# One-core cross-attention block: the small passes of four engines moved between the steps of the attention loop

## What is computed

```python
def layer_norm(x, w, b):
    mu = jnp.mean(x, axis=-1, keepdims=True)
    var = jnp.mean(jnp.square(x - mu), axis=-1, keepdims=True)
    return (x - mu) * jax.lax.rsqrt(var + EPS) * w + b
residual = hidden_states
x = layer_norm(hidden_states, ln1_w, ln1_b)
q = (x @ q_w + q_b)                       # (B, H, LQ, HD) after the turn; k, v from the context
scores = jnp.einsum('bhqd,bhkd->bhqk', q, k) * scale
scores = jnp.where(mask, scores, mask_value)
attn = jax.nn.softmax(scores, axis=-1)
out = jnp.einsum('bhqk,bhkd->bhqd', attn, v)
out = out @ cproj_w + cproj_b             # heads side by side again
hidden = out + residual
residual = hidden
y = layer_norm(hidden, ln2_w, ln2_b)
y = jax.nn.gelu(y @ fc_w + fc_b, approximate=True)
return residual + (y @ proj_w + proj_b)
```

## Time and profile before

| | us |
|---|---|
| median of 3 runs | 833.96 (829.85, 833.96, 834.24) |
| the profiled execution, whole | 829.58 |
| its span, first to last instruction | 827.8 |
| projections, until the first s2 of the loop | 154.3 |
| attention loop | 298.7 |
| MLP | 375 |

### The profile page before, as it was taken

The page is one execution under the profiler, slowest core; times in us unless marked ns, Lnnn a source line. Parts: engine busy times, 40 slices in busy tenths (PEclk is TensorE's granted clock), DMA queues, the critical chain, the costliest instruction groups (busy, mean ns, idle before and its releaser), DMA issues.

```text
span 827.8 us, 10032 instructions
## 1 busy us (share of the span) xinstructions
PE 772.7 (93%) x3728; PEld 525.8 (64%) x3728; DVE 454.9 (55%) x967; ACT 274.2 (33%) x483; POOL 311.9 (38%) x190
## 2 busy tenths in 40 slices
PE   6999999889889888988898899999999999999998
PEld 5878887433225322533352688888888888888886
DVE  6764345788775788767778745633323332332222
ACT  4434232366654555356545300111112111111010
POOL 2634040257864675477646534532001110112000
PEclk9999999799989998989999999999999999999999
DMA  8647296848545764464523253104000400020001
GB/s 305 229 154 276 92 291 180 273 127 206 128 104 128 197 162 104 128 178 104 128 100 104 65 166 128 64 1 153 1 0 1 152 1 0 1 73 31 0 1 51
DMA packets 58288, 94.85 MB, mean 115 GB/s; under 512 B 5920, under 2 KB 14372, under 8 KB 58240
## 3 DMA queue, kind: packets, MB, share of 16 engines
q1 hardware_dynamic: 58096, 94.19, 38.6%
q10 hardware_dynamic: 144, 0.02, 0.0%
HBM read 68.89 MB, written 25.18 MB: 114 GB/s over the span
## 4 chain that ended last, share of the span: by engine, by line
PE 74%; DVE 15%; ACT 5%; issue 3%; DMA 2%; POOL 1%; SPq 0%; DVEq 0%; ACTq 0%
PE ps L424 20%; PE ps L426 20%; PE ps L425 20%; DVE ps L902 6%; PE ps L561 4%; PE ps L546 4%; ACT Pt L732 3%; PE ps L530 3%; PE ps L515 2%; DVE BIG L942 1%; DVE R L921 1%; PE ps L483 1%; DVE R L1014 1%; DVE R L913 1%; DMA BIG<-mT 1%
## 5 line engine op out<-in xcount | busy, mean ns | idle before, releaser
L732 ACT ACTIVATE Pt<-ps 128x512 f32<-128x512 f32 x256 | 135.4, 599 | 112.2 <-PE ps L530 112.1
L1056 DVE CAST HR<-R 128x512 fp32r<-128x512 f32 x52 | 24.2, 465 | 184.7 <-ACT R L766 184.7
L530 PE MATMUL ps<-BIG 98*128 98x512 f32 x256 | 98.5, 468 | 16.0 <-ACT Pt L732 11.0
L530 PEld LDWEIGHTS ps<-BIG 98*128 98x128 f32 x256 | 45.3, 198 | 98.0 <-ACT Pt L732 66.4
L766 ACT ACTIVATE R<-ps,cols 128x512 f32<-128x512 f32 x52 | 35.8, 689 | 205.5 <-PE ps L426 205.5
L902 DVE CUSTOM_DVE_ANT_0 ps<-ps,FU 128x512 f32<-128x512 f32 x128 | 84.4, 721 | 25.3 <-PE ps L515 25.2
L902 DVE CUSTOM_DVE_ANT_0 ps<-ps,BIG 128x512 f32<-128x512 f32 x128 | 84.4, 721 | 20.0 <-PE ps L515 19.9
L1179 POOL TENSOR_TENSOR R<-Pt 128x1024 f32<-128x1024 f32 x20 | 48.2, 2424 | 76.3 <-ACT Pt L732 76.2
L424 PE MATMUL ps<-BIG,HR 128*128 128x512 f32 x192 | 75.0, 390 | 2.1 <-DVE HR L1058 2.1
L424 PE MATMUL ps<-YT,BIG 128*128 128x512 f32 x192 | 75.8, 395 | 0.0
L426 PE MATMUL ps<-YT,BIG 128*128 128x512 f32 x192 | 74.8, 390 | 0.0
(11 more groups left out here) (121 smaller groups left out, 1395.8 us busy)
## 6 DMA issues: line engine op xcount, KB each, us to landing
BIG<-qs SPq DMA_DIRECT2D x62, 256.0 KB, 3.0
BIG<-ks SPq DMA_DIRECT2D x62, 256.0 KB, 3.0
ks<-BIG SPq DMA_DIRECT2D x32, 256.0 KB, 2.0
qs<-BIG SPq DMA_DIRECT2D x32, 256.0 KB, 6.3
R<-hd SPq DMA_DIRECT2D x28, 256.0 KB, 4.2
R<-in_x SPq DMA_DIRECT2D x16, 256.0 KB, 4.4
hd<-R SPq DMA_DIRECT2D x16, 256.0 KB, 2.0
RW<-in_fc_w SPq DMA_DIRECT2D x16, 256.0 KB, 2.8
```

What stands on the lines that cost most here:

```text
L530: eng.matmul(bk, K_[0:98, j, kc * 128:(kc + 1) * 128], Q_[0:98, j, :], start=True, stop=True).then_inc(S["p_ra"], 1)
L732: eng.activation(Pt[:, r, j % 2, :], bank(bank_a(("s2", i, j))), ACT.Exp, scale=SCALE).then_inc(S["a_ra"], 1)
L1056: eng.tensor_copy(HR[:, n, 0, :], g).then_inc(S["v_hh"], 1)
```

## The change

- ACT's output passes of stack s - 2 go from behind the exponentials of kc = 1 to kc = 2, between the second and the third exponential; those of stacks 0, 4, 8, 12 go from kc = 3 to kc = 0 of the next stack.
- PE: pv goes ahead of the sums and of all that follows; `cproj` and `y_turn` go from the end of a step to ahead of its third s2. The four c-products of a batch are in steps i % 16 = 8 to 11 (before 7 to 10), the y-turns in steps 44, 45, 47, 49 (before 44, 48, 52, 56).
- `EARLY` goes from 6 to 8: two more s1 groups (all of stacks 0 and 1) stand in the projections of b = 3, with their maxima; the maxima of stack q are turned at kc = 0 of stack q - 1 (before kc = 2), those of stack 0 one projection earlier. SP's loads of stack 2, of masks and of leads shift accordingly.
- The quotient of an odd stack below 15 goes to a second buffer (`prod`), which lies over columns 3072 to 3583 of BIG, and `divide_c` waits for the `out_low` of two stacks before. Slab 3 of the MLP weights uses the same columns, so its split waits for the `out_low` of stack 13. `divide_c` of stack 14 moves into step 63.
- The four normalisations of LN2's first batch go from DVE (steps 35, 37, 39, 41) to POOL (36, 38, 40, 42), statistics one step later. The copies of the c-weights go from steps 1 to 4 to steps 4 to 7; slabs 2 and 3 from steps 58 and 60 to 60 and 61; slab 5 behind the first GELU's split. On POOL `out_low`, `y_low` and `x_add` move, the last by two steps.

The diff, cut to its core:

```diff
+        with nc.sbuf_tensor("BF", [128, 24576], F32) as BF:
+            pass
         BIG = sb("BIG", [128, 24576], R)
...
+        def prod(s):
+            return BF[:, 3072:3584] if s % 2 and s < NS - 1 else R1[:, 3, :]
...
-        EARLY = 6
+        EARLY = 8
+        EARLY_K, EARLY_Q = {0: 3, 1: 4, 3: 5}, {1: 6, 3: 7}
...
-        YTURN = (44, 48, 52, 56)
+        YTURN = (44, 45, 47, 49)
...
-        SLABS = (56, 57, 58, 60)
+        SLABS = (56, 57, 60, 61)
...
(sync)
+                if b == 3:
+                    load_lead(2)
...
-                if b == 3:
-                    load_stack(2)
                 for g in range(4):
-                    if b == 3 and g == 2:
+                    if b == 3 and g == 1:
                         store_max(0)
...
+                if kc == 0 and s + 3 < NS:
+                    load_lead(s + 3)
                 if kc == 0 and s >= 1 and s + 2 < NS:
                     load_stack(s + 2)
                 if i in TURNS:
                     store_max(TURNS[i])
-                if i == 0:
+                if i == 1:
+                    load_stack(2)
+                if i == 2:
                     for n in range(1, 4):
                         load_mask(n)
-                if kc == 3 and s + 3 < NS:
-                    load_lead(s + 3)
...
(tensor, projections of b = 3)
                         proj_V(b, [c])
-                        if c % 2:
-                            s1(c // 2)
+                        if c:
+                            s1(c - 1)
...
-                    if b == 3 and g % 2:
-                        s1(2 + g // 2)
+                    if b == 3 and g in EARLY_K:
+                        s1(EARLY_K[g])
...
-                    if b == 3 and g == 2:
+                    if b == 3 and g == 1:
                         turn_maxima(0)
...
-                    if b == 3 and g % 2:
-                        s1(4 + g // 2)
+                    if b == 3 and g in EARLY_Q:
+                        s1(EARLY_Q[g])
...
(tensor, loop)
                 if i in GROUPS:
                     s1(GROUPS[i])
+                if i >= 2:
+                    pv(i - 2)
                 if kc == 2 and s:
                     sums(s - 1)
-                if i >= 2:
-                    pv(i - 2)
+                if i >= 20 and 8 <= i % 16 < 12:
+                    bk = ring_b(RB[("cp", b - 1, i % 16 - 8)])
+                    cproj(b - 1, i % 16 - 8, bk).then_inc(S["p_rb"], 1)
+                if i in YTURN:
+                    k = YTURN.index(i)
+                    pe.wait_ge("g_nm", 4)
+                    bk = ring_b(RB[("yt", k)])
+                    y_turn(0, k, bk).then_inc(S["p_rb"], 1)
                 s2(i, 2)
                 s2(i, 3)
-                if i >= 20 and 7 <= i % 16 < 11:
-                    bk = ring_b(RB[("cp", b - 1, i % 16 - 7)])
-                    cproj(b - 1, i % 16 - 7, bk).then_inc(S["p_rb"], 1)
-                if i in YTURN:
...
(scalar, loop)
                 if kc == 1 and s >= 1:
                     copy_pv(s - 1)
+                if kc == 2 and s >= 2 and (s - 2) % 4:
+                    split_out(s - 2)
+                if kc == 0 and s >= 3 and (s - 3) % 4 == 0:
+                    split_out(s - 3)
                 exp(i, 2)
                 exp(i, 3)
-                if kc == 1 and s >= 2 and (s - 2) % 4:
-                    split_out(s - 2)
-                if kc == 3 and s >= 2 and (s - 2) % 4 == 0:
-                    split_out(s - 2)
...
-                if 1 <= i <= 4:
+                if 4 <= i <= 7:
                     act.wait_ge("d_wc", 16)
...
(vector)
                 dve.wait_ge("a_pv", s + 1)
-                if s:
-                    dve.wait_ge("g_al", s)
-                eng.tensor_tensor(R1[:, 3, :], R1[:, 0, :], R1[:, 2, :], ALU.mult).then_inc(S["v_at"], 1)
+                if s >= 2:
+                    dve.wait_ge("g_al", s - 1 if s < NS - 1 else s)
+                eng.tensor_tensor(prod(s), R1[:, 0, :], R1[:, 2, :], ALU.mult).then_inc(S["v_at"], 1)
...
                 elif f < 4:
                     dve.wait_ge("p_rb", RB[("s1", 16 * NS - 1)] + 1)
+                    if f == 3:
+                        dve.wait_ge("g_al", 14)
...
                 if kc == 0 and s >= 2:
                     divide_c(s - 2)
+                if i == NI - 1:
+                    divide_c(NS - 2)
...
-                if 35 <= i < 43 and i % 2:
-                    norm(HN, 0, 4, (i - 35) // 2)
                 if i in SLABS:
                     split_slab(SLABS.index(i))
-            divide_c(NS - 2)
             split_slab(4)
-            split_slab(5)
...
                 if i == 0:
+                    split_slab(5)
                     divide_a(NS - 1)
...
(gpsimd, loop)
+                if kc == 3 and s >= 2 and (s - 2) % 4:
+                    out_low(s - 2)
+                if kc == 1 and s >= 3 and (s - 3) % 4 == 0:
+                    out_low(s - 3)
+                if i - 2 in YTURN:
+                    y_low(0, YTURN.index(i - 2))
                 if kc % 2:
...
-                if kc == 2 and s >= 2 and (s - 2) % 4:
-                    out_low(s - 2)
-                if kc == 0 and s >= 3 and (s - 3) % 4 == 0:
-                    out_low(s - 3)
-                if i in YTURN:
-                    y_low(0, YTURN.index(i))
-                if i >= 12 and (i - 12) % 16 in (0, 2, 4, 6):
-                    x_add((i - 12) // 16, (i - 12) % 16 // 2)
-                if i == 34:
+                if 14 <= i < 60 and (i - 14) % 16 in (0, 2, 4, 6):
+                    x_add((i - 14) // 16, (i - 14) % 16 // 2)
+                if i > 60:
+                    x_add(3, i - 61)
+                if i == 35:
                     root(0, 4)
+                if i in (36, 38, 40, 42):
+                    c = (i - 36) // 2
+                    pool.wait_ge("g_rs", 5)
+                    eng.tensor_scalar(HN[:, c, :], HN[:, c, :], mv[:, 0, c, 0:1], rs[:, 0, c:c + 1],
+                                      ALU.subtract, ALU.mult).then_inc(S["g_nm"], 1)
```

More of the change, by code:

```diff
@@ L362, in _ @@
                     store_max(TURNS[i])
-                if i == 0:
+                if i == 1:
+                    load_stack(2)
+                if i == 2:
                     for n in range(1, 4):
                         load_mask(n)
-                if kc == 3 and s + 3 < NS:
-                    load_lead(s + 3)
-                if i >= 20 and 7 <= i % 16 < 11:
-                    c = i % 16 - 7
+                if i >= 20 and 8 <= i % 16 < 12:
+                    c = i % 16 - 8
                     sp.wait_ge("v_rb", RB[("cp", b - 1, c)] + 1)
                     eng.dma_start(hd[4 * (b - 1) + c], R2[:, c, :]).then_inc(S[f"d_hd{c}"], 16)
-                if 9 <= i % 16 < 13:
-                    c = i % 16 - 9
+                if 10 <= i % 16 < 14:
+                    c = i % 16 - 10
                     if b == 0:
@@ L378, in _ @@
                     eng.dma_start(R2[:, c, :], xv[b][:, c, :]).then_inc(S[f"d_xr{c}"], 16)
-                if i == 27:
+                if i == 28:
                     ln2_load(0)
@@ L680, in _ @@
                     k = f - 11
-                    pe.wait_ge("v_nm", 16 + 4 * (b + 1) + 4)
+                    pe.wait_ge("v_nm", 16 + 4 * (b + 1))
                     if b == 0 and k < 2:
@@ L735, in split_out @@
                 b, g = divmod(s, 4)
-                ta = R1[:, 3, :]
+                ta = prod(s)
                 act.wait_ge("v_at", s + 1)
@@ L820, in _ @@
                         act.wait_ge(f"d_qk{n}", 256)
-                    eng.activation(WC[0][:, i - 1, :], R2[:, i - 1, :], ACT.Copy).then_inc(S["a_wc"], 1)
+                    eng.activation(WC[0][:, i - 4, :], R2[:, i - 4, :], ACT.Copy).then_inc(S["a_wc"], 1)
             split_out(NS - 2)
@@ L972, in _ @@
                 if b == 3:
-                    for j in range(8):
+                    for j in range(12):
                         maximum(j)
@@ L980, in _ @@
                     qk_low(b, g, 0)
-                    if b == 3 and g % 2:
+                    if b == 3 and g in EARLY_K:
                         for j in range(4):
-                            maximum(4 * (2 + g // 2) + j)
+                            maximum(4 * EARLY_K[g] + j)
                 if b == 0:
@@ L991, in _ @@
                         x_affine(1)
-                    if b == 3 and g % 2:
+                    if b == 3 and g in EARLY_Q:
                         for j in range(4):
-                            maximum(4 * (4 + g // 2) + j)
+                            maximum(4 * EARLY_Q[g] + j)
             for i in range(NI):
@@ L1118, in out_low @@
                 pool.wait_ge("a_ah", s + 1)
-                low(AT[1][:, s % 4, :], R1[:, 3, :], AT[0][:, s % 4, :], "g_al")
+                low(AT[1][:, s % 4, :], prod(s), AT[0][:, s % 4, :], "g_al")
             def x_add(b, c):
```

30 lines of the change are left out of this document (12 added, 18 removed).

## The result

| | median us | lowest, highest | runs | ratio to the kernel before, 95% |
|---|---|---|---|---|
| before | 834.04 | 828.59, 837.12 | 15 | |
| changed | 822.11 | 818.52, 829.51 | 15 | 0.9886 [0.9855, 0.9917] |
| changed, measured again (same_again) | 822.75 | 818.80, 829.20 | 12 | 0.9905 [0.9873, 0.9937] |

The change makes the kernel 1.1% faster, where 2.3% were forecast (815 us); the time lies inside the range of 806 to 829. The profiled execution took 818.52 us (span 816.7) against 829.58 before: 11.1 us less, where the sum said 16.9.

What follows compares the result with a forecast made beforehand. No engine is full in the attention loop; waits between engines within a step bound it. Savings 8.0 + 6.2 + 2.3 - 1.3 + 1.7 = 16.9 us, 812.7 against the profiled 829.58; forecast 815, range 806 to 829.

Steps and rivals of the forecast that it cites:

- The plain stacks: Attention loop: with output passes later and pv ahead of sums, each plain stack should take stack 2's 14.99 us.
- Product steps: Steps with a c-product, now mid-step: 5.8 us, 7.5 with sums, 24.9 per stack of four; no gain, no loss.
- the y-turns: Stacks 11 and 12, turns moved mid-step: steps 44 to 47 take 18.7 us; both stacks 34.4 against 36.67, 2.3 saved.
- the tail's stall: Stack 15: slab 3's split waits for stack 13's low part, delaying step 63's s2; some 3 us more, bounds 0 and 6.
- the MLP: MLP start: one slab only is split before the first GELU's split, so PE's 1.70 us wait goes; 0 to 2.5 saved.
- The copies of the c-weights: Moved to steps 4 to 7: hidden in DVE's gaps for 0.7 us more than before; stacks 0 and 1 30.4 for 31.1.
- The start: Loop start: 2.80 us transfer wait goes, yet first s1 0.8 us later; with stacks 0 and 1 nothing, -1 to +2.
- turned maxima: Moved from a stack's third step to the first, where DVE's quotient work covers the 0.2 us turn: no gain or loss.
- GpSimd's normalisation: Stacks 9 and 10: four normalisations move from DVE to GpSimd, taken at 1.28 us each, bounds 0.54 and 2.26.
- A: Rival: half the gain, waits taking new places (GpSimd beside product stacks, longer tail); 822 or 826 us; chance 0.17.
- B: Rival: GpSimd's passes hold DVE's quotient multiplications, 14.6 us back, 827 to 831, no change; 0.10 with other ways.
- C: Rival: PE's third steps granted clock 0.76 whatever the order, 7.25 us for 4.76, 845 us; 0.11 with a far worse tail.

Runs made afterwards that it cites:

- wc_early: Changed kernel with only the copies of the c-weights put back from steps 4 to 7 to steps 1 to 4; 818.31 us, 0.9844 of the kernel before.
- turn_third: Changed kernel with only the turned maxima put back into the third step of the same stack; 830.19 us, 0.9990 of the kernel before.
- turn_third_back: Changed kernel with the turned maxima back in the third step, the output passes back and the sums ahead of pv again; 842.68 us, 1.0139 of the kernel before.

## Why the prediction was right and wrong

- **Right in size.** The plain stacks take 15.0 us, taken from stack 2. Product steps 5.8 to 6.2 and 7.5, the y-turns 18.4 for 18.7 us, the tail's stall where it was put, the MLP 2.8 us shorter for 1.7 forecast.
- **The term that failed.** The copies of the c-weights were "hidden in DVE's gaps for 0.7 us more than they were", and stacks 0 and 1 were to take 30.4 us. A held subtraction took 2.90 us instead, in step 5, whose maxima step 6 waits for. Steps 6 to 8 took 6.0 us more than before, 5.9 of which came back in wc_early. So the moved copies, put at a gain of 0.7 us, cost about 6: as much as the 5.8 us by which the sum's 16.9 lies over the 11.1 of the profiled execution. The start below (1.4 us worse) and all other parts (1.3 us better) cancel. The price was in the rows: POOL's adds of 2.38 us, and a multiplication of 0.69 us that took 1.66 right after DVE had waited for GpSimd. I used it for the quotients and not for this moved instruction.
- **The start, 1.4 us late.** Two more s1 groups and their maxima put the loop's first s1 at 157.59, not 156.2; the range of -1 to +2, which was for the whole start with stacks 0 and 1, would have held this by itself, but not the copies on top.
- **The mechanism was half right.** "The passes go behind the second exponential of the third step, and pv goes ahead of the sums" was given the gain of the plain stacks, and of the turned maxima the prediction said "nothing" twice: it left the wait of the sums on the third step's first exponential, where it had been. The runs show three sufficient cures. Moving the turn changes which eviction the sums' seat waits for, and with the passes and the order put back it alone gives 4.8 us. It also issues the maxima's transfer sooner, and ahead of the LN2 loads; without it there is a stall of 3.6 to 5.7 us in the one step where they meet. That the gain of stacks 3 to 6 came out right (7.8 us for 8.0) is in part luck: the two named moves are enough, as turn_third shows, but the kernel that ran did not need them.
- **GpSimd's normalisation** took 2083 ns (mean of four), where I took 1.28 and had 2.26 as the bound:

```profile
L1205 POOL TENSOR_SCALAR HN<-HN,mv,rs 128x512 f32<-128x512 f32 x4 | 8.3, 2083 | 0.0
```

No wait of PE in stacks 9 and 10 is put down to it. These two stacks took 42.7 us for 40.9, and stacks 7 and 8 30.7 for 31.5. Most of the 1.8 us stands in one step of stack 9, in which DVE's small operation for the variances took 1.40 us where its median is 0.17, ahead of maxima for which PE waits 1.83 us; the forecast had 0.7 us for the variances. No run has removed it, so this cause is read from the trace only:

```profile
314.42 0.51 PE L523 MATMUL ps<-BIG 32*128 32x512 f32 x4 [1.83 <-DVE mx L910]
...
310.36 1.40 DVE L863 TENSOR_SCALAR ve<-mv 128x4 f32<-128x4 f32 x1
```

- **The rivals.** A came true in size (its 822 us was met) and in kind, for a wait took a new place, but not in the places that it named: the product stacks' neighbours and the tail came near the forecast, and GpSimd's adds did it by holding DVE's copy of a c-weight. B (held quotients) did not: the multiplications into R have a median of 0.69 us, those into the second buffer 0.98, and none of it reaches PE in a plain stack. The Trainium skill's page "SBUF — State Buffer", section "Who interferes with whom", says that the port pair which VectorE shares with GpSimd is an exclusive lock, and that a VectorE instruction with two inputs in SBUF contends with a GpSimd instruction that reads SBUF. The trace agrees with it for L1042 (0.64 us free, 2.90 beside two adds), and it was the right rule for the wrong instruction. C (the clock falls in the third step whatever the order) did not hold for the plain stacks 3 to 5: 4.8 us in every kernel with a cure. But in same_again the third steps of stacks 9 and 13 had 0.74 and 0.73, 3.2 of the 6.8 us between the two profiled executions.

Not tried: one of the three cures put into the kernel before by itself, and the change's normalisation on GpSimd undone alone.

## What to carry to other kernels

When an instruction is moved, ask of every engine what stands behind its new place and what runs beside it then; a price of "hidden" needs the row of the same kind at its held length, not its free one. In a ring of buffers, taking a seat out changes which eviction every later seat waits for: count the seats back before giving the gain to something else. And try each part of a change alone as well as all of them undone, for one part put back shows nothing when the others cover for it.

## What was not expected of the hardware

The PE wait of 2.28 us in step 6 cost 6.0 us in all. After it the granted clock was 0.50 through the next step of 5.01 us and 0.63 through the one after, of 5.15 us; in wc_early the same two take 3.50 and 3.30 us at 1.00. After the 2.12 us wait at the loop's start the first step has 0.56. Yet of the waits of 0.93, 0.94 and 0.96 us in the third steps of stacks 3 to 5 of turn_third_back the second stands in a step at 1.00 and the others in steps at 0.77, so waits of that size may or may not cost. The spread of one kernel's runs goes with the clock too: those of the changed kernel with a mean granted clock of 0.981 took 818.5 and 818.6 us, with 0.977 820.8 to 822.1, with 0.969 828.7 to 829.5. The same kernel's third steps of stacks 9 and 13 took 4.8 us in one profiled execution and 6.3 and 6.4 in another, though the PE waits ahead of them were the same in both (1.83 and 1.84 us in stack 9, 0.94 and 0.93 in stack 13).

GpSimd took 2.08 us for a `tensor_scalar` of 128x512 with two per-partition operands, longer than its addition of two tensors of that size (1.28 us).
